# Weight loads and shared-row stores moved from SyncE's DMA queue to ScalarE's in a mixture-gated attention kernel

## What is computed

```
xn = layernorm(x)
s  = attention(xn)            # causal, one head of 512, own gamma and beta, o_proj, residual xn
g  = silu(ffn(xn))            # see below
out = x + s * g

ffn(x):  gates = softmax(x @ router_w.T); the best 2 of 8 experts, renormalised
         routed = sum over the 2 experts of  gate * (silu(x @ wg_e) * (x @ wu_e)) @ wd_e     # wg, wu 512 x 352, wd 352 x 512
         shared = (silu(x @ sg) * (x @ su)) @ sd                                             # 512 x 704, 704 x 512
         return routed + shared
```

## Time and profile before

| what | us |
|---|---|
| median of 3 runs | 1178.71 |
| lowest, highest | 1176.1, 1180.24 |
| profiled execution, its own time | 1181.12 |
| its span, first to last instruction | 1179.4 |
| mean granted TensorE clock in the span | 0.988 |

### The profile page before, as it was taken

The page is one execution under the profiler, slowest core; times in us unless marked ns, Lnnn a source line. Parts: engine busy times, 40 slices in busy tenths (PEclk is TensorE's granted clock), DMA queues, the critical chain, the costliest instruction groups (busy, mean ns, idle before and its releaser), DMA issues. The chain is left out here.

```text
span 1179.4 us, 21143 instructions
## 1 busy us (share of the span) xinstructions
PE 1145.7 (97%) x6608; PEld 630.4 (53%) x6609; DVE 566.9 (48%) x1168; ACT 471.0 (40%) x824; POOL 422.5 (36%) x659
## 2 busy tenths in 40 slices
PE   8999979999999999999999999999999999999996
PEld 5555545555555555555555555554454454454442
DVE  6866656576648521121221221221377477477475
ACT  5543423444423222232232232233655645645652
POOL 2262323332200122222222222221764764754753
PEclk8999989999999999999999999999999999999998
DMA  9888987899733589988899787786766776665363
GB/s 283 219 203 223 253 164 198 191 223 240 191 78 80 102 155 201 204 200 203 204 206 190 176 177 177 182 176 172 139 161 192 159 166 185 161 165 165 116 157 93
DMA packets 371458, 210.22 MB, mean 178 GB/s; under 512 B 308912, under 2 KB 322232, under 8 KB 371392
## 3 DMA queue, kind: packets, MB, share of 16 engines
q1 hardware_dynamic: 360560, 173.68, 63.9%
q0 software_dynamic: 10800, 35.69, 11.9%
q10 hardware_dynamic: 32, 0.02, 0.0%
HBM read 89.31 MB, written 46.01 MB: 115 GB/s over the span
## 5 line engine op out<-in xcount | busy, mean ns | idle before, releaser
L676 PE MATMUL pair<-arena 128*128 (+2 forms) x3240 | 507.1, 313 | 2.6 <-DMA arena<-arena 1.4
L676 PEld LDWEIGHTS pair<-arena 128*128 128x128 f16 x3240 | 316.4, 98 | 186.0 <-issue 3.9
L683 PE MATMUL bank<-arena 128*128 (+1 forms) x1215 | 287.4, 382 | 12.8 <-DMA arena<-arena 12.8
L683 PEld LDWEIGHTS bank<-arena 128*128 128x128 f16 x1215 | 119.1, 98 | 142.2 <-DMA arena<-arena 12.2
L1522 DVE SCALAR_TENSOR_TENSOR arena<-pair,slot_unit,arena 128x352 f32<-128x352 f32 x71 | 41.4, 584 | 270.8 <-ACT arena L1438 244.9
L1438 ACT ACTIVATE arena<-pair,slot_unit 128x352 f32<-128x352 f32 x71 | 39.3, 554 | 207.3 <-PE pair L676 180.1
L1201 POOL COPY arena<-token_of 128x1 uint32 (+1 forms) x71 | 13.0, 183 | 279.0 <-issue 97.8
L1810 PE MATMUL bank<-arena 128*128 128x512 f16 x432 | 100.0, 384 | 2.3 <-DVE arena L1966 2.3
L1797 PE MATMUL pair<-arena 128*128 128x512 f16 (+3 forms) x576 | 97.5, 326 | 0.6 <-ACT arena L1854 0.6
L1203 POOL DMA_INDIRECT arena<-xn_rows,arena x71 | 71.0, 1000 | 55.6 <-POOL arena L1201 52.5
L1782 PE MATMUL bank<-arena 128*128 128x512 f16 x384 | 86.0, 379 | 1.6 <-PEq L1025 1.6
(11 more groups left out here) (186 smaller groups left out, 1178.6 us busy)
## 6 DMA issues: line engine op xcount, KB each, us to landing
slot_rows<-arena SPq DMA_DIRECT2D x71, 256.0 KB
arena<-in_L_attn_x_dram SPq DMA_DIRECT2D x64, 256.0 KB, 3.5
xn_rows<-arena SPq DMA_DIRECT2D x32, 260.0 KB, 2.8
shared_rows<-arena SPq DMA_DIRECT2D x32, 256.0 KB
arena<-shared_rows SPq DMA_DIRECT2D x32, 256.0 KB
out_dram<-arena SPq DMA_DIRECT2D x32, 256.0 KB, 2.1
arena<-in_L_ffn_wg_dram SPq DMA_DIRECT2D x32, 176.0 KB, 3.1
arena<-in_L_ffn_wu_dram SPq DMA_DIRECT2D x32, 176.0 KB, 3.3
```

The lines of the kernel that those rows point to most:

```text
L676: last = pe.matmul(bank[:, 0:width], xt[:, a, c, :], weights(c, b, col, width), start=(c == 0 and i == 0), stop=(c == KC - 1 and i == 2))
L683: last = pe.matmul(bank[:, :], ht[:, a, c, :], weights(c, b), start=(start and c == 0 and i == 0), stop=(stop and c == HC - 1 and i == 2))
```

## The change

The loads of the routed weights and the stores of the shared rows are issued by ScalarE, so in ScalarE's own DMA queue. All turns, the loads and stores of token tiles, the fold's pieces and all of the later parts stay with SyncE. Only the first chunk of `wg`/`wu` and the first of `wd` are still loaded by SyncE. On ScalarE the load of chunk `i + 1` stands just ahead of `in_high(i)`, the load of `wd` for step `s + 1` behind the second `h_high` of step `s`, and the store of a shared tile just behind its `y_copy`.

```
+            def load_in(eng, i):
+
+                u, e, r = i % 2, i // KC, i % KC
+                wait(eng, in_lo, i - 1)
+                for n, w in enumerate((wg, wu)):
+                    eng.dma_start(in_stage[u][:, n * H:(n + 1) * H], w[e, r * P:(r + 1) * P, :]).then_inc(in_loaded[u], 16)
+
+            def load_down(eng, i):
+
+                e, r = i // HC, i % HC
+                wait(eng, down_lo, i)
+                rows = down_rows(r)
+                eng.dma_start(down_stage[0:rows, :], wd[e, r * P:r * P + rows, :]).then_inc(down_loaded, 16)
...
@@ sync @@
-                    def load_in(i):
...
-                    def load_down(s):
...
-                    def store_y(t):
-                        n = t if t < 0 else (USUAL + list(DEFERRED))[t]
-                        sp.wait_ge(y_ready, t + 1)
-                        sp.dma_start(shared_rows[n * P:(n + 1) * P, :], y_out).then_inc(y_stored, 16)
...
                     fold_sync(sp)
-                    for i in in_chunks(0)[:1]:
-                        load_in(i)
+                    load_in(sp, 0)
+                    load_down(sp, 0)
                     sp.wait_ge(pads, 2)
                     for s in range(NT):
...
                         if s > 0:
                             turn_h(2 * s - 1)
-                        load_down(s)
-                        for i in in_chunks(s)[1:]:
-                            load_in(i)
-                        if s > 1:
-                            store_y(s - 2)
                         turn_h(2 * s)
                         if s > 0:
                             store_fold(sp, s - 1)
-                        for i in in_chunks(s + 1)[:1]:
-                            load_in(i)
                     turn_slot_x(1)
                     turn_h(2 * NT - 1)
-                    store_y(NT - 2)
                     slot_tile(0)
-                    store_y(NT - 1)
                     for j in range(1, 4):
                         slot_tile(j)
...
@@ scalar @@
                     def in_high(i):
+                        if i + 1 < E * KC:
+                            load_in(act, i + 1)
                         if i == 20:
                             act.wait_ge(fold_stored, 2 * KC * 16)
...
                         nc.scalar.activation(y_out, y_bank[t % 2][:, :], ACT.Copy, scale=Y_SCALE).then_inc(y_ready, 1)
+                        n = (USUAL + list(DEFERRED))[t]
+                        act.wait_ge(y_ready, t + 1)
+                        act.dma_start(shared_rows[n * P:(n + 1) * P, :], y_out).then_inc(y_stored, 16)
...
                         h_high(2 * s + 1, 1)
+                        if s + 1 < E * HC:
+                            load_down(act, s + 1)
                         if s == 0:
                             split_hi(act, IN_SPLITS + 2)
```

## The result

The change made the kernel slower: 1202.12 us (median of 4 runs, 1197.65 to 1204.23) against 1178.53 for the kernel before in the same session, ratio 1.0198, 95% interval 1.0179 to 1.0217. The forecast was 1177.8, its range ended at 1186. The profiled execution of after has a span of 1201.5 us, 22.1 more than before.

A forecast was written before the change was run, and what follows sets the result against it. TensorE, busy 97% of the span, was taken as the bound. Hand-over -1.4, bias store -1.5 and two-tile steps +2.0 sum to -0.9: 1181.12 becomes 1180.2 us, the median 2.4 lower, so 1177.8, range 1171.5 to 1186.

The forecast's parts named there:

- The two-tile steps: +2.0: Six steps passing two token tiles: half a pair delays the turn of h, +2.0 us, bounds -4.3 to +7.9.
- The bias store: -1.5: Step of the bias store: the wg/wu pair behind it moves elsewhere, -1.5 us, at most -3.1, at least 0.
- The four small waits: 0: Four L683 waits, 3.4 us in all: no change, bounds -3.4 to +3.2 us.
- 10 us at the 1.2 GHz level: Window 150 to 200 us: mean clock 0.90 read as 10 us at 1.2 GHz after the long idle, instead of 2.4.
- rival 2: The loads overtake the turns in the six two-tile steps: +7.9 there, +6.5 in all, 1185 us, chance 0.18.
- the hand-over: Passage to the routed tiles: with the last store on ScalarE, slot tile 3's turn goes sooner, -1.4 us, bounds -1.4 to 0.
- ScalarE's side 0: Two-chunk steps: 2.7 us of added issuing hides in ScalarE's 3.5 us of idle time, cost 0.
- rivals 3 and 4: 3: ScalarE becomes the bound, 1212 us, chance 0.05; 4: its transfers end up behind the same backlog, 1177.3, chance 0.04.
- SyncE's side 0: SyncE gives up 54 us of issuing, but its turns wait for other engines anyway, so gain 0.
- The rule beside the rows: Two skill sections: issuing engines save only issue time (-1.4 alone), or queues are served round-robin (loads overtake turns); neither shown.

The follow-up runs named there:

- the order of before: Against the kernel after: a semaphore holds ScalarE's wd, pair and y issues behind SyncE's turns of h, as in the kernel before; 1179.5 us, ratio 1.0016.
- the early order: Against the kernel before: SyncE issues everything in one queue, in the order in which the changed kernel's issues fell; 1193.7 us, ratio 1.0133.
- ScalarE's later issues: Against the kernel after: ScalarE issues pairs behind h_high of each unit, y behind h_high of the next step's first unit, wd unmoved; 1189.9 us, ratio 1.0108.

## Why the prediction was wrong

*The step that failed is "The two-tile steps: +2.0".* Its mechanism was right, its size was not. At the ends of these steps TensorE waits 24.10 - 9.44 = 14.7 us longer, and the nine matmuls behind the waits took 1.55 + 1.9 + 1.9 us at the lower clock less the 1.38 that stood behind 94.35: together +18.6, where even the upper bound was +7.9. Four parts were missing from that bound:

- It priced three of the six steps, those that end at 94, 129 and 239 (the third had the term of the bias). The fourth and the sixth had no wait before (their down products ran on time at 206.03 and 273.14), and got no term; with 2.85 and 4.04 us of waiting and the slow matmuls behind them they cost 10.3 of the 18.6. The first, for which a growth was forecast, shrank from 2.88 to 2.13 and lost its slow matmuls.
- It counted a pair and a wd; the y store (256 KB, as large as the wd) also went ahead of the turn.
- It held the first turn of x of a step as fixed. That turn had only 0.73 us of lead; the load of x that feeds it stands in the step before, and its landing went from 3.5 to 4.5 us. In the fifth step that made the chain 2.1 us later.
- It put no half clock on the new stalls. The stalls of 2.85 us and more at the ends of these steps were each followed by 1.55 to 1.9 us of it.

Slack was measured at the last link alone (3.4 and 3.8 us against a landing of 3.4); the turn of x ahead of it had 0.73 us.

*"The bias store: -1.5"* was right about the pair and wrong for the change as a whole. With the pairs alone on ScalarE, the time from the bias issue to TensorE's restart fell from 169.66 - 150.77 = 18.89 us to 168.12 - 151.75 = 16.37, by 2.5, and the wait from 6.56 to 4.14. In the kernel after, that time is 174.99 - 156.07 = 18.92, so nothing came out, and the wait grew by 3.44 us besides, because the bias itself went out later:

```profile
153.05 0.69 DVE L241 BATCH_NORM_STATS2 moments<-arena 128x6 f32<-128x512 f32 x1 [3.90 <-DMA arena<-in_L_attn_x_dram]
...
155.68 3.78 PE L676 MATMUL pair<-arena 128*128 128x360 f16 x24
156.07 0.57 SPq L426 DMA_DIRECT2D bias_row<-bias_v  x1
```

It is issued 0.39 us behind the start of the step's first unit, where before it was 3.02 ahead (150.77 against 153.79). VectorE stood 3.90 us waiting for a load of x; behind that in its program are the low part of h, then on SyncE the turn of it and the bias. These 3.44 us are part of the 14.7 above. Moving the bias itself removed most of the stall.

*"The four small waits: 0"*: 0.86, 2.90, 1.45 and 0.40 us are now outside the two-tile steps, where before 0.97, 0.30 and 0.73 stood in the same early part: +3.6, just above the bound of +3.2. The fourth small wait of before, 1.32 us, is at 809.23, out of reach of the change.

*Readings:* of the "10 us at the 1.2 GHz level" in the bias step, some 4 lie inside the idle time itself (the granted clock is 0.50 from 166 to 175 us), so the matmuls lost less than that reading suggests; no term used it. The end of the range, 1186, is a little above rival 2's own 1185.

*Right:* the hand-over, its 1.42 us gone at the place named; ScalarE's side 0. ScalarE's issues took 0.33 us (wd, y, wg) and 0.47 (wu, once 2.14) at the median, and rivals 3 and 4 did not occur. SyncE's side 0: with the order of before, SyncE is rid of the same issues, and the time is 1.9 us longer, not shorter. Rival 2's sign in the profile, six waits of 1 us or more on L683, is there.

*The rule beside the rows.* The Trainium skill, "DMA: Bandwidth & Descriptors", section on issuing engines not being separate DMA queues, says that issuing from several engines saves only issue time. The run with the order of before agrees: 1.0016. Its section on queues and rings has the queues served in turn; the trace fits where a turn of h, issued at an unchanged point of the step with other bytes in the second queue, is used 6.34 us later instead of 3.82; no run shows the rounds themselves. The two together are the result: no gain, and the order that one queue had kept was lost.

## What to carry to other kernels

A single queue is also a schedule: with wd, y and the pair issued ahead of it in the same queue, the turn of h went out 7.19 us into the step instead of 5.33. Before moving transfers to a second queue, list for each the critical transfers that it used to stand behind, and let it wait for them in the new place too; here the issues held back by one counted semaphore cost 1.9 us, and the same issues running free 23.6. Measure slack at every link of the chain that feeds the turn, not at the last; price every step of the kind, also those that are on time; and price a stall with the matmuls at half clock that can follow it. Put a store of many single numbers (10.2 us to land here) where nothing critical stands behind it: moving the bias row and the last store was worth 6 us, with an earlier load of x 11.

## What was not expected of the hardware

- The costs of the three moved parts were not additive: 2.6 us for the pairs alone, 23.6 for all three.
- In the fifth two-tile step, early bytes delayed a transpose in two ways: in its own queue by its start (7.19 us into the step instead of 5.33, used 3.86 us later), in another queue by the time from its start to its use (6.34 us instead of 3.82, from an unchanged start).
- An issue on ScalarE took 0.33 us where the same store took 0.43 on SyncE.
- In the kernel after, nine matmuls behind a pause of 2.13 us took 2.12 us, behind 2.85 us (at 213.80) 3.67, but behind 2.90 us (at 58.33) 2.10: the length of the pause alone does not tell the clock.

Open: wd or y alone were not tried; how the loss divides between the late load of x and the bytes ahead of the turn of h, why the early order costs 16 us in one queue and 23.6 in two, and why the leads were as bad with ScalarE's later issues as in after, were not isolated.
